# An early-fusion block on one core: router steps moved, both norms applied by VectorE, expert stores overlapped, and the experts' second product in rounded pieces

## What is computed

```python
h = h + attn(_layernorm(h))       # 12 heads of 16, rope, causal, a sink per head
xf = _layernorm(h)
top_p, top_i = jax.lax.top_k(softmax(xf @ gate_w.T), 2)     # 8 experts
# cap = ceil(1.25 * 2 * N / 8) = 4560 rows per expert, in order of arrival
z = 2.0 * buf
z = z * jax.lax.rsqrt(jnp.mean(z * z, -1, keepdims=True) + EPS) * norm_w[:, None, :]
g, u = jnp.split(jnp.einsum('ecd,ehd->ech', z, w13), 2, axis=-1)      # hidden 512
y = buf + jnp.einsum('ech,edh->ecd', jax.nn.silu(g) * u, w2)
h = h + sum over a row's two experts of weight * y
```

## Time and profile before

| | us |
|---|---|
| median of 3 runs (lowest, highest) | 3116.91 (3115.43, 3157.16) |
| the profiled execution | 3111.47 |
| its span, first to last instruction | 3109.3 |
| TensorE busy | 2852.4 (92%) |
| GpSimd busy | 2019.5 (65%) |
| VectorE busy | 1827.3 (59%) |
| ScalarE busy | 1497.5 (48%) |

### The profile page before, as it was taken

The page is one execution under the profiler, slowest core; times in us unless marked ns, Lnnn a source line. Parts: engine busy times, 40 slices in busy tenths (PEclk is TensorE's granted clock), DMA queues, the critical chain, the costliest instruction groups (busy, mean ns, idle before and its releaser), DMA issues.

```text
span 3109.3 us, 62400 instructions
## 1 busy us (share of the span) xinstructions
PE 2852.4 (92%) x20432; PEld 2539.9 (82%) x20432; DVE 1827.3 (59%) x5319; ACT 1497.5 (48%) x3736; POOL 2019.5 (65%) x2070
## 2 busy tenths in 40 slices
PE   1899999999999999999999985999999999999997
PEld 0788888888888888888878875989898989888997
DVE  2466766676676766677766753444444545444544
ACT  0455555555555555555555553444443444344433
POOL 2567877777777777777777742555565555555555
PEclk9899999999999999999999997999999999999999
DMA  6354445433444433444433303343333343433343
GB/s 182 131 165 156 152 162 172 146 101 101 114 115 115 108 95 104 115 115 115 110 96 102 84 23 74 54 68 48 68 54 68 47 68 54 67 49 66 54 67 44
DMA packets 205961, 297.49 MB, mean 96 GB/s; under 512 B 88374, under 2 KB 167675, under 8 KB 205874
## 3 DMA queue, kind: packets, MB, share of 16 engines
q1 hardware_dynamic: 82994, 243.82, 27.4%
q0 software_dynamic: 122880, 52.55, 12.0%
HBM read 201.73 MB, written 93.90 MB: 95 GB/s over the span
## 4 chain that ended last, share of the span: by engine, by line
PE 32%; issue 22%; POOL 19%; DMA 14%; DVE 6%; ACT 4%; POOLq 1%; DVEq 1%; SPq 0%; ACTq 0%
DMA out<-arena,who 13%; POOL out L1460 10%; PE bank L861 6%; POOL moe_rows L1281 5%; PE bank L979 3%; PE bank L927 3%; DVE arena L1442 3%; PE bank L952 2%; PE bank L954 2%; PE bank L905 2%; PE bank L1029 2%; POOL rstd L706 2%; PE bank L963 1%; PE bank L852 1%; PE bank L929 1%
## 5 line engine op out<-in xcount | busy, mean ns | idle before, releaser
L1460 POOL DMA_INDIRECT out<-arena,who x320 | 596.1, 1863 | 187.4 <-issue 183.2
L1281 POOL DMA_INDIRECT moe_rows<-row,slot x256 | 293.2, 1145 | 349.0 <-issue 324.8
L570 DVE TENSOR_REDUCE top<-bank 114x2 f32<-114x456 f32 (+1 forms) x576 | 352.9, 622 | 240.9 <-PE bank L921 153.4
L1418 ACT ACTIVATE arena<-bank 128x456 f32<-128x456 f32 x320 | 174.9, 547 | 602.4 <-PE bank L1409 600.8
L685 POOL TENSOR_TENSOR arena<-arena 112x896 f32<-112x896 f32 x192 | 402.2, 2096 | 44.4 <-DMA arena<-in_x 44.4
L1432 PE MATMUL bank<-prob,arena 128*114 128x192 f32 x2560 | 429.3, 326 | 0.0
L1432 PEld LDWEIGHTS bank<-prob,arena 128*114 128x114 f32 x2560 | 412.2, 178 | 0.0
L1424 DVE TENSOR_TENSOR arena<-bank,arena 128x456 f32<-128x456 f32 x320 | 201.5, 630 | 209.3 <-ACT arena L1418 207.3
L1449 POOL TENSOR_TENSOR rms<-rms,minus_half 114x4 f32<-114x4 f32 x82 | 85.3, 1040 | 345.3 <-DVE rms L1347 345.3
L725 POOL TENSOR_TENSOR qk<-rot_c,qk 114x384 fp32r<-114x384 f32 x256 | 253.7, 1014 | 44.4 <-ACT qk L746 44.4
L547 ACT ACTIVATE pieces<-bank 64x456 fp32r<-64x456 f32 x384 | 209.2, 545 | 149.3 <-PE bank L905 147.1
(11 more groups left out here) (167 smaller groups left out, 6971.3 us busy)
## 6 DMA issues: line engine op xcount, KB each, us to landing
arena<-in_x SPq DMA_DIRECT2D x64, 2352.0 KB, 11.6
arena<-moe_rows SPq DMA_DIRECT2D x82, 363.4 KB
moe_rows<-filler SPq DMA_DIRECT2D x20, 1453.5 KB
out<-h SPq DMA_DIRECT2D x64, 171.0 KB
out<-arena,who POOLq DMA_INDIRECT x320, 5.0
arena<-in_w_t SPq DMA_DIRECT2D x9, 512.0 KB, 6.7
arena<-in_w_t SPq DMA_DIRECT2D x18, 256.0 KB, 7.1
moe_rows<-row,slot POOLq DMA_INDIRECT x256, 4.1
```

The source lines that it names most:

```text
L570: nc.vector.tensor_reduce(dst, src, AX.X, ALU.max).then_inc(maxed[k], 1)
L1281: nc.gpsimd.indirect_dma_start(out=moe_rows[0:SLOTS, :], out_offset=bass.IndirectOffsetOnAxis(ap=slot[at.par][:, 2 * t + k:2 * t + k + 1], ...
L1460: nc.gpsimd.indirect_dma_start(out=out[:, :], out_offset=bass.IndirectOffsetOnAxis(ap=who[par][:, s:s + 1], axis=0), in_=ys[par][:, s, :], ...
```

## The change

In the attention stage: `norm1_apply` and `norm2_apply` move from ScalarE to VectorE, as subtract-and-multiply with the mean and the inverse deviation; VectorE adds eps; of `inverse_std` the power alone stays on GpSimd. `choose`, `assign` and `weigh` stand earlier in VectorE's step, the second rotation and the poolings later; TensorE's `turn_xn`, `turn_xf`, `gate_logits` and `rank` stand earlier; GpSimd takes the second norm ahead of the first fold. In the expert stage: the hidden rows and `w2` are split into high and low fp32r parts too (`high_hid` on ScalarE, `low_hid` on VectorE, two more weight pieces), and the second product is three fp32r products for each fp32 one. `take_numbers` comes behind `weigh_rows`; `add_rows` waits for earlier stores at an expert's first tile only; filler rows are out of bounds and are dropped. The weight pieces are spread over the last two pairs. Semaphores `gate_up` and `hid_made` become single counters, and a few small buffers go.

```diff
+            nc.vector.tensor_scalar(var[:, :], mv[:, :, 1:2].rearrange("p a b -> p (a b)"), LN_EPS, None,
+                                    ALU.add).then_inc(step, 1)
...
+        def norm1_apply(dve, at):
+            dve.wait_ge(ln1_step, 4 * (at.b + 1))
+            wait(dve, xn_turned, at.b)
+            for t in range(2):
+                ins = nc.vector.tensor_scalar(xn[:, t, :, 0:C], h[at.par][:, t, :].rearrange("p (c k) -> p c k", c=2),
+                                              mv1[:, t, 0:1], rstd1[:, t:t + 1], ALU.subtract, ALU.mult)
...
-            nc.gpsimd.tensor_tensor(var[:, :], spread2, ln_eps[:, 0:2], ALU.add).then_inc(step, 1)
-            pool.wait_ge(step, 6 * at.b + 3)
             nc.gpsimd.tensor_tensor(rstd[:, :], var[:, :], minus_half[:, 0:2], ALU.pow).then_inc(step, 1)
-            pool.wait_ge(step, 6 * at.b + 4)
-            nc.gpsimd.tensor_tensor(scaled[:, :], mean, rstd[:, :], ALU.mult).then_inc(step, 1)
...
-            ring("S1 C1 S2")
+            ring("S1 C1")
             if a:
                 turn_xn(pe, a)
-            ring("C2 S3")
+            ring("S2 C2 S3")
+            if t:
+                attend(pe, t, 0)
             if a:
                 make_qk(pe, a, 0)
-            if t:
-                attend(pe, t, 0)
-            ring("C3 S4")
             if z:
                 turn_xf(pe, z)
+            ring("C3 S4")
             if a:
                 make_qk(pe, a, 1)
-            ring("C4 S5")
             if z:
                 gate_logits(pe, z)
-            ring("C5 S6")
+            ring("C4 S5 C5 S6")
             if t:
                 attend(pe, t, 1)
-            ring("S7 C6")
             if z:
                 rank(pe, z)
-            ring("S8 C7 C8")
+            ring("S7 C6 S8 C7 C8")
...
                 if a:
                     inverse_std(pool, a, norm1)
-                if p:
-                    fold_image(pool, p, 0)
                 if z:
                     inverse_std(pool, z, norm2)
                 if p:
+                    fold_image(pool, p, 0)
                     fold_image(pool, p, 1)
...
+        PIECES = ((0, 1), (2, 3), (4,), (5,))
...
-            hold(dve, y_weighted, n - 1, held)
+            hold(dve, y_weighted, n, held)
...
+        def high_hid(act, n, j):
+            act.wait_ge(hid_made, 4 * n + j + 1)
             if j == 0:
+                wait(act, down, n)
+            nc.scalar.activation(hid2[:, j, 0, :], hid[:, j, :], ACT.Copy).then_inc(hid_high, 1)
+
+        def low_hid(dve, n, j):
+            dve.wait_ge(hid_high, 4 * n + j + 1)
+            nc.vector.tensor_tensor(hid2[:, j, 1, :], hid[:, j, :], hid2[:, j, 0, :].bitcast(fp32),
+                                    ALU.subtract).then_inc(hid_low, 1)
...
-                pe.wait_ge(hid_made[j], n + 1)
+                pe.wait_ge(hid_low, 4 * n + j + 1)
                 for s in range(SUB):
-                    ins = nc.tensor.matmul(bank[6 + s // 2][0:TT, D * (s % 2):D * (s % 2 + 1)], hid[:, j, TT * s:TT * (s + 1)],
-                                           w_dn[e_par][:, j, :], start=(j == 0 and s % 2 == 0), stop=(j == 3),
+                    for part, (h_part, w_part) in enumerate(((0, 0), (0, 1), (1, 0))):
+                        ins = nc.tensor.matmul(dst, hid2[:, j, h_part, at], w_dn2[e_par][:, j, w_part, :],
+                                               start=(j == 0 and s % 2 == 0 and part == 0), stop=(j == 3 and part == 2),
...
-            pool.wait_ge(y_weighted, n + 1)
             pool.wait_ge(numbered, n + 1)
-            if par:
-                hold(pool, added[0], 16 * SUB * (pair + 1), held)
-            else:
-                hold(pool, added[1], 16 * SUB * pair, held)
+            if first:
+                wait(pool, added[0], 16 * SUB * pair)
+                wait(pool, added[1], 16 * SUB * pair)
+            hold(pool, y_weighted, n + 1, held)
...
-                    in_=ys[par][:, s, :], in_offset=None, bounds_check=TOKENS + ROWS - 1, oob_is_err=True,
+                    in_=ys[par][:, s, :], in_offset=None, bounds_check=TOKENS - 1, oob_is_err=False,
```

More of the change, by code:

```diff
@@ L1160, in step_vector @@
             maxima("3")
+            if z:
+                choose(dve, z)
+            if a:
+                rotate(dve, a, 1)
+            maxima("4")
             if p:
                 pool_image(dve, p, 1)
-            if a:
-                rotate(dve, a, 1)
-            maxima("4 5")
+            maxima("5")
             if z:
-                choose(dve, z)
+                assign(dve, z)
+                weigh(dve, z)
             maxima("6")
@@ L1472, in pair_of @@
                     pair = e * PT + k
-                    last = isinstance(k, int) and k == PT - 1
+                    first, last = (isinstance(k, int) and k == i for i in (0, PT - 1))
+                    late = k - (PT - 2) if isinstance(k, int) and k >= PT - 2 else None
                     for par in range(2):
-                        tile(2 * pair + par, e, e_par, par, pair, last)
+                        tile(2 * pair + par, e, e_par, par, pair, first, last, late)
                 pair_of(0)
@@ L1507, in _, with tile @@
                 load_rows(sp, par, par)
-            def tile(n, e, e_par, par, pair, last):
+            def tile(n, e, e_par, par, pair, first, last, late):
                 sp.wait_ge(z_made, n + 1)
@@ L1531, in _, with tile @@
             inverse_rms(pool, 1)
-            def tile(n, e, e_par, par, pair, last):
+            def tile(n, e, e_par, par, pair, first, last, late):
                 inverse_rms(pool, n + 2)
-                add_rows(pool, n, par, pair)
+                add_rows(pool, n, par, pair, first and not par)
             over_tiles(pool, tile)
@@ L1575, in _, with tile, weights @@
             square_rows(act, 0, 0, 0)
-            round_z(act, 0)
+            round_za(act, 0)
+            round_zb(act, 0)
             square_rows(act, 1, 1, 0)
-            def tile(n, e, e_par, par, pair, last):
+            def tile(n, e, e_par, par, pair, first, last, late):
                 n1, par1, pair1 = ahead(n, par, pair)
+                def weights(j):
+                    for piece in pieces_of(late, par, j):
+                        round_expert(act, e + 1, 1 - e_par, piece)
                 silu(act, n, 0)
                 weigh_x(act, n, par)
-                for j in range(1, 4):
-                    silu(act, n, j)
-                    piece = piece_of(last, par, j)
-                    if piece is not None:
-                        round_expert(act, e + 1, 1 - e_par, piece)
-                round_z(act, n + 1)
+                silu(act, n, 1)
+                high_hid(act, n, 0)
+                high_hid(act, n, 1)
+                silu(act, n, 2)
+                weights(2)
+                high_hid(act, n, 2)
+                silu(act, n, 3)
+                round_za(act, n + 1)
+                high_hid(act, n, 3)
+                round_zb(act, n + 1)
+                weights(3)
                 square_rows(act, n + 2, par, pair + 1)
```

166 lines of the change are left out of this document (80 added, 86 removed).

## The result

| | before | after |
|---|---|---|
| runs beside each other, us | 3116.68 (3115.43 to 3157.16) | 3452.73 (3398.14 to 3463.15) |
| ratio, 95% interval | | 1.0945 [1.0747, 1.1142] |
| profiled execution: time, span | 3111.47, 3109.3 | 3459.82, 3458.0 |
| steady attention step (e.g. after: 1111.97 to 1146.15) | 27.36 | 34.13 |
| expert stage, mean tile | 14.8 | 14.2 |

The kernel is 9.5% slower where the prediction said 1.7% faster; 3452.73 lies far outside its range.

The account below looks back on a forecast made before the run. Bounds: an attention-step loop through TensorE, VectorE's router weights, GpSimd and ScalarE; in expert tiles, TensorE and the store loop. Span 3109.3 + 22 (attention) - 72 (experts) + 1 (first weights) = 3060, time 3062, stated as 3065; range 2980 to 3140.

Parts of the forecast that it names:

- the price of the second apply: Attention stage, VectorE: each norm apply of two 114x192 operations taken at 0.6 us, bounded above by 1.1.
- The 1.2 for the weights: Attention stage, VectorE: the router's weights, seven small operations, take 1.2 us together, now ahead of the shift.
- rival D: Expert stage: landings grow with two tiles' stores in flight, so stores don't overlap; tile 14.7, 3130 us; chance 0.08.
- the chain: Attention step: choose starts at 12.2 us, VectorE runs without rest, shift turns at 21.9, 5.78 follow; step 27.7.
- the stall at the first norm: Attention stage: TensorE's stall ahead of the transpose of the normed rows, about 1.6 us a step, goes.
- Pace 0.100: Expert stage: 48 second-product records at 0.10 us each, 4.8 a tile, 0.4 less than before; tile 13.8.
- what is left of stalls: Expert stage: TensorE's remaining stalls add 0.1 us to the 13.8 us tile, making 13.9.
- The term for the stores: Expert stage: stores overlap and VectorE takes numbers after weighing, so its landing waits fall under 1 us each.
- B: Attention stage, VectorE's chain: applies at 1.1 us and ring waits not side by side; step 28.9, 3188 us; chance 0.10.
- A: Attention stage, mid-step: VectorE reaches the shift as early as before; step 25.9, 2947 us, half 2990; chance 0.24.
- C: Expert stage: second product follows its columns, 0.081 a record, 3.9 us a tile; tile 12.9, 2990 us; chance 0.05.

Follow-up runs that it names:

- run 14: Run 9's kernel with the token counter in PSUM and eight TensorE products that nobody reads ahead of the third attend: 3099.15 us, ratio 0.997.
- run 9: Changed kernel, but VectorE's second norm apply reads the inverse deviation from a PSUM copy as a second tensor: 3274.0 us, ratio 1.050.
- 13: Run 9's kernel plus eight TensorE products that nobody reads, ahead of the third attend: 3215.24 us, ratio 1.036.
- run 3: Changed kernel plus eleven TensorE products that nobody reads, ahead of the turn of the second norm's rows: 3368.36 us, a single run.
- run 2: Changed kernel, but ScalarE applies the second norm, with a shift that VectorE makes in one small operation: 3263.26 us, ratio 1.049.
- run 4: Changed kernel, but GpSimd starts the first image fold only after VectorE has applied the second norm: 3439.9 us, a single run.
- run 10: Old attention stage with the changed expert stage, but each tile's stores wait again for those of the tile before: 3061.7 us, ratio 0.983.
- run 12: Run 9's kernel with the token counter kept in PSUM: 3139.91 us, ratio 1.010.

## Why the prediction was wrong

**The sum, term by term.** The step grew by 6.8 us, forecast 0.35. By steps with the clock whole, 27.36 before: the new order itself makes 27.95 (run 14; +0.6), the held-up small operation 28.77 (run 9's and 13's whole-clock steps; +0.8), the held-up apply 30.84 (run 3; +2.1), and the clock 34.13 (+3.3). The parts are differences between kernels that each carry a small addition (the copy to PSUM of 0.15 us, the products nobody reads), so each is good to a few tenths. In runs 9 and 13 the small operation is the counter. In the changed kernel itself the counter takes 0.17 and another is held up in its place, the first of the weights (median 0.93 for 0.16 before), until GpSimd's L730 ends at 1136.20:

```profile
1135.28 0.94 DVE L655 TENSOR_SCALAR gden<-gexp 114x2 f32<-114x2 f32 x1
```

```profile
1132.17 4.03 POOL L730 TENSOR_TENSOR qk<-rot_c,qk 114x384 fp32r<-114x384 f32 x4
```

Together with the experts' stage: (34.02 - 27.69) x 63 distances, by the mean step, = +399, and -48, is +351; the spans differ by 3458.0 - 3109.3 = 349.

**Step that failed 1: the price of the second apply.** "I take 0.6", bounded by 1.1. The nearest row, L532, reads from PSUM; the apply moves one tensor from SBUF to SBUF. That it stood beside the folds was in my own chain (power at 5.9, fold from there to 8.0), but the bound was taken from an operation of another kind. A clue stood in the trace of before, in a row that I hadn't read: all instances of one line, with their shortest, median and longest time in ns.

```profile
L577 DVE TENSOR_TENSOR shift<-top,sink_tok x64: 207/599/620, 107.2 to 1842.9; 114x48 f32<-114x48 f32 x64
...
L656 DVE TENSOR_SCALAR token<-token x64: 168/169/170, 166.7 to 1882.9; 114x2 f32<-114x2 f32 x64
```

L577 has two SBUF inputs and stands beside GpSimd's work: 48 numbers a row take 207 ns or three times that. L656, clear of GpSimd's tensor work, takes 169 each time. A median far from the shortest time, for a fixed shape, was the sign. The runs show 0.67 alone, 2.25 and 2.42 beside one fold, 4.00 beside two, 0.74 with an operand in PSUM. The 4.00 are two holds, not one: no single operation of L534 took more than 2.12, one fold's length. The 1.2 for the weights failed in the same way: they were priced clear of GpSimd, where L643 stood, and took 2.1 (1135.28 to 1137.37).

The Trainium skill has this rule, under "SBUF — State Buffer", SBUF: two separate sides: VectorE's second port pair is GpSimd's only one, an exclusive lock, and a VectorE operation in a two-port mode, or with two SBUF inputs against a GpSimd instruction that reads SBUF, has to wait until GpSimd's whole instruction is over, or the other way round. The trace agrees with the lock: apply and folds end 0.13 us apart. Run 2's L535, with two SBUF inputs, agrees as well. In which mode the apply ran, no row shows. The prediction did weigh that lock, but against GpSimd's stores (rival D), not against its folds, and in the other direction.

**Step that failed 2: the clock.** The forecast took every TensorE duration at the full clock and priced idle time at its length. The profile of before showed a few stretches at half (68 us in all in the attention stage), a sign that the clock could fall here. In the changed kernel TensorE idles 2.3 us of the first 12.13, and half clock follows in every step. That idle time is the cause, and not the other way round, runs 3, 13 and 14 show: products nobody reads make the kernel faster. One stretch of 3.4 us costs 1.7 (30.45 against 28.77 in run 9); the same products show both levels there, first at 1.00, then at 0.50:

```profile
1320.00 1.47 PE L865 MATMUL bank<-w_qkv,xn_t 97*114 97x192 f32 x8
1321.30 0.82 PE L989 MATMUL bank<-ident,y_t 128*114 128x128 f32 x6
```

```profile
1349.05 2.77 PE L865 MATMUL bank<-w_qkv,xn_t 97*114 97x192 f32 x8
1351.61 1.49 PE L989 MATMUL bank<-ident,y_t 128*114 128x128 f32 x6
```

**What was right: the chain.** I had 12.2 for choose, 21.9 for the shift's turn, 5.78 behind it and 27.7 in all. In run 14, a step starts at 1025.86 and the next at 1053.80:

```profile
1035.98 1.52 PE L856 MATMUL bank<-w_qkv,xn_t 97*114 97x384 f32 x4 [0.52 <-DVE rot_s L552]
1037.33 0.88 PE L1026 MATMUL bank<-gate,xf_t 96*114 96x8 f32 x8
...
1047.99 0.42 PE L933 MATMUL bank<-ident,shift 114*128 114x114 f32 x2
...
1053.80 0.44 PE L947 MATMUL bank<-pieces 128*115 128x456 f32 x1
```

Choose starts 12.5 in (1038.37), the shift turns at 22.1, 5.8 are left, and the wait for the rotation ahead of the second query/key product is 0.52 where I had 0.7. So the new order, even without the held-up operations and the clock, is no gain: it takes away the stall at the first norm and lengthens VectorE's chain to the shift by as much. The stall ahead of `turn_xn` is gone in the changed kernel, as forecast.

**The experts' stage.** Pace 0.100 as taken, and the median tile is 13.9, where 13.8 was said. The size was off: -48 for -72. The mean tile is 14.2 for 13.9, because ten of the 80 tiles, one or two an expert, still take 15.6 to 17.8 us (16.2 to 18.4 before); in or beside them TensorE waits 1.2 to 2.4 us at a stretch, mostly for gated rows (L1425). The prediction had put what is left of stalls at 0.1 a tile and those long ones as gone. The term for the stores was mis-sized and its reason was wrong: 0.5 us a tile for their overlap, and run 10 has nothing for it. VectorE's waits for landings fell from 79 to 8, and to 13 without the overlap, so it isn't the overlap that took them away; what is left for it is that the numbers are now taken behind the weighing, which no run has alone. How the 48 us divide between that move and the product in pieces was not tried.

**The rivals.** B was of the right sign and named the right place (VectorE's chain, dearer applies), but its price for the applies had the same bound as the forecast's, so it reached 3188. A, C and D don't show.

## What to carry to other kernels

Before a VectorE operation is put beside GpSimd's tensor work, look at its form, not its size: an elementwise one with all its tensors in SBUF may cost what GpSimd's running instruction has left; an operand in PSUM kept it free here, and the reductions were never held up (L494, 1.07 us either way). Where TensorE is near full use, count each new wait twice: once for its length, and once for the clock that may fall behind it; the changed `PEclk` row was a result of the waits here, not their cause. And when two parts of a change are independent, as both stages are here, time one alone: it would have been a gain of 1.5%.

## What the runs showed of the hardware

- Beside GpSimd's tensor work an operation on 114x2 numbers took 0.93 us instead of 0.17 (the counter, run 9), another 1.79 instead of 0.15 (L535, run 2; 0.15 is its shortest): how long it is held follows GpSimd's instruction, not its own size.
- Being held up is booked as busy time of the VectorE instruction. The views of waits don't name it; a group's mean that leaves its own shortest time does (L534: 1916 ns in the mean of 128, where the two of run 4's row take 0.66 together).
- Taking 0.76 us from one tiny instruction (run 12) gave 134 us, 2.4 of the median step, since half clock fell with it.
